# Relation-aware attention on eight cores: each transposed copy waits for its own transposes and for the last reader of its buffer, instead of for the newest matmul

## The reference

```python
x = x + attn(layernorm(x)); x = x + moe(layernorm(x))

rel = jnp.tril(idx[:, None] - idx[None, :])
rk, rv = embk[rel], embv[rel]
att = einsum('bhtd,bhsd->bhts', q, k) * scale + einsum('bhtd,tsd->bhts', q, rk)
att = softmax(where(causal, att, -inf))
y   = einsum('bhts,bhsd->bhtd', att, v) + einsum('bhts,tsd->bhtd', att, rv)
return y.transpose(...).reshape(B, T, C) @ w_proj
```

## Time and profile before

| | us |
|---|---|
| timed runs | 5114.23 and 5203.96, median 5159.1 |
| the profiled execution | 5111.53 |
| its span, slowest core (core 1) | 5110.0 |
| the other cores' spans | 5060.6 to 5099.1 |
| TensorE busy | 3531.9 (69%) |
| VectorE busy | 1326.7 (26%) |
| ScalarE busy | 1309.4 (26%) |
| mean granted TensorE clock, share of full speed | 0.736 to 0.739 |

### The profile page before, as it was taken

How to read it: one execution, slowest core, us unless ns; L and a number is a source line. 1 busy time by engine, 2 the same in 40 slices (tenths; PEclk the granted TensorE clock), 3 DMA queues, 4 the chain that set the end, 5 groups by cost and what they waited for, 6 DMA issues and landing times.

```text
span 5110.0 us, 48667 instructions; the slowest of 8 cores (5060.6 to 5110.0 us)
## 1 busy us (share of the span) xinstructions
PE 3531.9 (69%) x16065; PEld 1578.7 (31%) x16065; DVE 1326.7 (26%) x2303; ACT 1309.4 (26%) x2274; POOL 213.5 (4%) x373
## 2 busy tenths in 40 slices
PE   0556557555675556665556612999999999999991
PEld 0222223222232222222222201444444444444440
DVE  0134432444433444434444211011001100110011
ACT  3423223323333322233322042211221122112110
POOL 1000000000001000000000001000000000000002
PEclk9855557555565555665555755999999999999995
DMA  5255444433335334433334413030303113030303
GB/s 127 60 114 121 116 101 81 125 114 107 110 92 135 108 107 115 110 102 105 110 114 116 135 56 70 9 66 1 66 1 66 34 33 66 1 66 1 66 1 127
DMA packets 455410, 415.89 MB, mean 81 GB/s; under 512 B 304464, under 2 KB 353632, under 8 KB 455160
## 3 DMA queue, kind: packets, MB, share of 16 engines
q1 hardware_dynamic: 409856, 336.72, 23.9%
q0 software_dynamic: 45312, 76.06, 9.1%
HBM read 264.16 MB, written 157.29 MB: 82 GB/s over the span
## 4 chain that ended last, share of the span: by engine, by line
PE 56%; DMA 12%; issue 11%; DVE 10%; ACT 6%; SPq 5%; POOL 1%; DVEq 0%; ACTq 0%; POOLq 0%
PE ps_v L61 17%; PE ps_h L61 17%; PE ps_s L61 10%; PE ps_y L61 8%; DMA prevh<-prev_sb 5%; SPq L61 5%; DVE ps_s L61 4%; DVE attT_sb L61 4%; PE ps_t L61 2%; DMA rel_sb<-prevh 2%; DMA xt_sb<-x 2%; ACT prev_sb L61 1%; ACT xn_sb L61 1%; DMA xt_sb<-x_spill 1%; DMA bt_sb<-bmath 1%
## 5 line engine op out<-in xcount | busy, mean ns | idle before, releaser
L61 PE MATMUL ps_v<-w_sb,h_sb 128*128 128x512 bf16 x4096 | 889.2, 379 | 34.1 <-ACT h_sb L61 34.1
L61 PE MATMUL ps_h<-xn2T,w_sb 128*128 128x512 bf16 x4096 | 892.1, 380 | 29.5 <-DMA w_sb<-w 29.5
L61 ACT ACTIVATE h_sb<-ps_h,b1c_sb 128x512 bf16<-128x512 f32 x512 | 351.9, 687 | 1459.6 <-PE ps_h L61 1459.6
L61 PE MATMUL ps_y<-attT_sb,vaug_sb 128*66 128x128 bf16 x2176 | 350.1, 306 | 474.3 <-DVE attT_sb L61 474.3
L61 DVE SCALAR_TENSOR_TENSOR acc_sb<-ps_v,g_sb,acc_sb 128x512 bf16<-128x512 f32 x256 | 192.2, 751 | 1649.2 <-PE ps_v L61 1649.2
L61 ACT ACTIVATE att_sb<-ps_s,cst_sb 128x512 bf16<-128x512 f32 x640 | 397.1, 686 | 692.3 <-DVE ps_s L61 572.5
L61 PEld LDWEIGHTS ps_v<-w_sb,h_sb 128*128 128x128 bf16 x4096 | 398.5, 98 | 524.8 <-issue 49.0
L61 PEld LDWEIGHTS ps_h<-xn2T,w_sb 128*128 128x128 bf16 x4096 | 401.4, 98 | 514.8 <-issue 33.4
L61 PE MATMUL ps_t<-eye_sb,att_sb 128*128 128x128 bf16 x2176 | 295.1, 295 | 342.8 <-DVE attT_sb L61 339.6
L61 DVE TENSOR_TENSOR ps_s<-ps_s,rel_sb 128x512 f32<-128x512 f32 (+3 forms) x624 | 387.5, 669 | 235.6 <-PE ps_s L61 126.9
L61 PEld LDWEIGHTS ps_y<-attT_sb,vaug_sb 128*66 128x66 bf16 x2176 | 233.7, 163 | 568.1 <-issue 568.1
(11 more groups left out here) (83 smaller groups left out, 1377.3 us busy)
## 6 DMA issues: line engine op xcount, KB each, us to landing
w_sb<-w POOLq DMA_DIRECT2D x64, 512.0 KB, 13.4
w_sb<-w POOLq DMA_DIRECT2D x128, 256.0 KB, 10.9
prevh<-prev_sb SPq DMA_DIRECT2D x80, 384.0 KB, 2.6
rel_sb<-prevh SPq DMA_DIRECT2D x80, 384.0 KB, 5.6
bmath<-att_sb SPq DMA_DIRECT2D x80, 384.0 KB, 2.9
xt_sb<-x SPq DMA_DIRECT2D x32, 512.0 KB, 4.1
rel_sb<-prevh SPq DMA_DIRECT2D x64, 256.0 KB, 4.1
xt_sb<-x_spill SPq DMA_DIRECT2D x32, 512.0 KB, 4.0
```

The source lines that it names most:

```text
L61: ins = getattr(h, method)(*args, **kw)
```

## The change

The waits of the copies into `attT_sb` are named one by one. Each call of `emit_trans` now has its count kept in `pvs`, each call of `emit_avs` in `avs_pe`. The copy of group q waits for the later of the transposes of group q (which it reads) and the AV matmuls of group q - 2 (which read the half of `attT_sb` that it writes). Before, it waited for all that TensorE had been given ahead of it, which from the second group on is the AV matmuls of group q - 1. The order of the instructions on every engine, their number and their operands are the same.

```diff
--- before.py
+++ after.py
@@ -607,20 +607,29 @@
                                                if (i % 4 == 0 and st == 0) else [])),
                                        incs=([(s_pe, 1)] if st == j1 - 1 else []))
 
-                            pv0 = emit_trans(0)
+                            pvs = {}
+                            avs_pe = {}
+
+                            def emit_avs2(q):
+                                emit_avs(q)
+                                avs_pe[q] = s_pe.n
+
+                            pvs[0] = emit_trans(0)
                             if ngr == 1:
-                                emit_copy(0, pv0)
-                                emit_avs(0)
+                                emit_copy(0, pvs[0])
+                                emit_avs2(0)
                             else:
-                                emit_trans(1)
-                                emit_copy(0, pv0)
+                                pvs[1] = emit_trans(1)
+                                emit_copy(0, pvs[0])
                                 for q4 in range(2, ngr):
-                                    emit_trans(q4)
-                                    emit_avs(q4 - 2)
-                                    emit_copy(q4 - 1, s_pe.n)
-                                emit_avs(ngr - 2)
-                                emit_copy(ngr - 1, s_pe.n)
-                                emit_avs(ngr - 1)
+                                    pvs[q4] = emit_trans(q4)
+                                    emit_avs2(q4 - 2)
+                                    emit_copy(q4 - 1,
+                                              max(pvs[q4 - 1], avs_pe.get(q4 - 3, 0)))
+                                emit_avs2(ngr - 2)
+                                emit_copy(ngr - 1,
+                                          max(pvs[ngr - 1], avs_pe.get(ngr - 3, 0)))
+                                emit_avs2(ngr - 1)
                             att_tr_done[ssl] = s_pe.n
                             vaug_guard[hpar] = s_pe.n
 
```

## The result

The changed kernel takes 4981.52 us in the median (4858.57 to 5228.1, 11 runs), the kernel before 5161.45 (5095.04 to 5421.03, 10 runs). The ratio is 0.9528, 95% interval 0.9467 to 0.9589: of 5111.5 us that is 241 us. The median is higher than the ratio suggests because in many executions of either kernel, the profiled one of the changed kernel (4955.64 us) among them, some cores run their expert and QKV stages at a lower clock for a time, so I read that profile on core 4, which did not, and the QKV boundaries of every profile on such undisturbed cores.

What follows compares the result with a forecast made beforehand. It took the attention stage to be set by latencies in a row, no engine full. Of 261 us of hops 206 counted, plus 8 for the clock: 5111.5 - 206 - 8 = 4897 us, range 4840 to 4985.

Steps and rivals of the forecast that it cites:

- The ping-pong, and its price by hops: Attention stage: later attT_sb copies and AV matmuls wait for each other in turn; shortening this saves 16.3 us a head.
- Strips 4 to 11 all count: Their AV work runs inside the main loop with no other wait between: 8.1 us a head, 130 us in all.
- Strips 12 and 13 are hidden at plain boundaries: At a head's end, behind the last exp, SP's queue of eight transposing loads is the path: nothing saved, 12 times.
- Strip 12 counts at the QKV boundaries, strip 13 is hidden there: Three places with a QKV stage between heads: strip 12 saves 3 x 2.05 = 6 us, strip 13 lies under prevh writes.
- Strips 14 and 15 count: Run inside the next head's prev stage, all in one row: 4.1 us, 15 times, 62 us.
- The clock: Attention stage: closer matmuls raise TensorE's granted clock in a further 2% of 1040 us; taken as 8 us.
- What would show it: Waits: attT_sb's for ps_y under 100 us, ps_y's about 270, ps_t's some 50 less; first expert matmuls about 210 sooner.
- That the clock opens for the whole stage: Rival, 4%: denser groups keep the attention stage at 2.4 GHz, 4500 us; 4700 if half of the time.
- That something else is late at once: Rival, 12%: prevh writes pace the prev stage, 4960 us; with half the main loop's gain lost to loads, about 5025.
- That copies and matmuls disturb each other in PSUM: Rival, 2%: each of 384 copies or the matmuls beside it slows; 0.54 us each cancels the gain, 0.8 gives 5214.

Runs made afterwards that it cites:

- The second copy alone: Changed kernel with the new wait only at the second copy of each strip, the later ones waiting as before; ratio 0.9766 to the kernel before.
- the wider buffer: Changed kernel with attT_sb twice as wide, room for four groups, so copies wait for their own transposes alone; median 4889.11 us of 4 runs.
- the early copies: Changed kernel with transposes and copies of a strip's groups 0 and 1 emitted ahead of the next strip's S matmuls and adds; ratio 0.9451.

## Why the prediction was right, point by point

The forecast was 4897 us, built on the profiled run; the median of 4981.52 lies inside the range of 4840 to 4985 by 3.5 us. That is luck, as the two medians are 180 us apart and the ratio's gain is 241: the ratio puts the forecast's 5111.5 at 4870, and the lowest timed runs are 4858.57 to 4874.11. The forecast gain was 214 us, the measured one 235 (profiles) to 241 (ratio). The direction, the mechanism and the size held; the forecast was some 10% short.

- *The ping-pong, and its price by hops.* Right to some hundredths: a three-group strip 1.29 us for 1.28, a four-group strip 2.12 for 2.1 (a3 at +3.10, forecast about +3.1), two-group strips 0.66 to 0.79 for 0.65 to 0.84. The second copy alone gave 0.86 for 0.87. One sum in it is off without a result: 0.41, 0.42 and 0.15 are 0.98 and not about 0.9, but two copies on end take 0.74 and not 0.83, and a1 waits for a0 in any case.
- *Strips 4 to 11 all count.* Right (146 us in the kernel that has only them), the 130 of the sum plus the clock.
- *Strips 12 and 13 are hidden at plain boundaries.* Right: 3.5 us in 12, as much as two profiles differ.
- *Strip 12 counts at the QKV boundaries, strip 13 is hidden there.* Right in the main: strip 12 gives 2.0 us each, strip 13 nothing clear at two boundaries and about 1 us at the third. Left out was that the QKV stage itself gets 0.4 to 0.6 us shorter in the changed kernel (44.4, 44.2 and 44.3 to 43.8, 43.8 and 44.0).
- *Strips 14 and 15 count.* Right at the plain boundaries, at 4.6 us for 4.1, and at the first and third QKV boundary. The half microsecond more was not taken apart; the clock is at 0.52 there in place of 0.50, which would fit. At the second QKV boundary it is wrong for strip 14, which is largely taken back by the prevh writes behind it.
- *The clock.* The direction was right, and its size is the term that was mis-sized: 8 us in the sum. It is 16 us in the loop and 3 at the end, some 20. I had spread it over the whole stage, and the 2% that it rests on was a guess that no row bears out. It came where AV groups run straight into a long run of other matmuls, and the timeline of before would have shown which strips those are (7 and 11), though not that the clock would rise there: it did not with the second copy alone, and seldom with the wider buffer. The granted clock of the whole stage went from 0.56 to 0.60 (core 4, 205 to 2590 us).
- *What would show it.* ps_y's wait about 270: 275.3. ps_t's 50 less: 32 less. attT_sb's wait under 100 us: 101.9, in 148 places. First expert matmuls 210 us sooner: 230 us in the mean of the cores (3152.5 to 2922.4).
- *The rivals.* That the clock opens for the whole stage: it does for single steps only. That something else is late at once: at one of the 15 boundaries only, by one to two us; with the early copies it is, at the bt_sb loads. That copies and matmuls disturb each other in PSUM: copies take 0.42 us beside running matmuls as before.

## What to carry to other kernels

A wait on "all that was issued so far" is free to write and can be a barrier between two engines that share a double buffer: name the producer and the last reader of the slot instead. Count the places of a wait in the table of waits; where the count is one of the code's own loop counts, every turn pays it, and the price is one hop read off the timeline. Then ask of each place what runs beside it: 49 us of the 261 that the hops add up to were hidden behind a DMA queue at the head's end. And where a gap closes right ahead of a long run of matmuls, look at the granted clock of that stretch as well: it is worth up to half of such a run, and it can go either way. A mean over cores or heads can hide two kinds of them, so look at each before you explain a difference in the mean.

## What the runs showed of the hardware

- The AV work of four strips in a row, with TensorE idle 0.68 us ahead of most of its groups of four matmuls, ran through 22.5 us at a granted clock of 0.50; with gaps of 0.25 us or none up to the rise (0.23 to 0.46 us behind it) the same work took 11.6 us at 0.78.
- A run of AV, bt_sb, S and transposing matmuls with no gap, 6.8 us long, stayed at 0.50 in one head of the kernel before; in another head of it, in the same step (strip 14 to 15), the clock was 0.50 through the eight bt_sb matmuls and 0.96 behind them. Which of the two comes was not taken apart.
- Copies from PSUM that follow each other in VectorE's queue take 0.74 to 0.76 us for two of 0.42.
- The transposing loads hold SP's queue 10.3 us for eight of them (10.26 in the kernel with the early copies, 10.32 in the earlier trace rows), while the engines' loop beside them became up to 1.5 us a strip shorter than in the changed kernel (9 to 10: 4.07 to 2.59).
